# A fused attention and expert layer on one core: layer norm with features on the partitions from the third group on, and the probabilities' transposes one step later

## The reference, cut to what matters

```python
def _layernorm(x, axis=-1, eps=1e-05):
    m = jnp.mean(x, axis=axis, keepdims=True)
    v = jnp.var(x, axis=axis, keepdims=True)
    return (x - m) / jnp.sqrt(v + eps)
...
    h = jax.nn.relu(x @ nm_w1 + nm_b1)
    m = h @ nm_w2 + nm_b2
    return _sliding_window_attention(m, q_w, q_b, k_w, k_b, v_w, v_b, WINDOW_SIZE)
...
    scores = jax.nn.sigmoid(gates.astype(jnp.float32))
    sel_scores = scores + expert_bias
    _, inds = jax.lax.top_k(sel_scores, K)
...
    hg = jnp.einsum('bsd,eid->bsei', x, w_gate)
    hu = jnp.einsum('bsd,eid->bsei', x, w_up)
    h = jax.nn.silu(hg) * hu
    ye = jnp.einsum('bsei,edi->bsed', h, w_down)
    y = jnp.einsum('bsed,bse->bsd', ye, combine).astype(x.dtype)
...
    xn = _layernorm(x, axis=-1)
    x = x + _L0_attn_ref(xn, ...) + _L0_ffn_ref(xn, ...)
```

## Time and profile before

| | before |
|---|---|
| median of 3 runs | 727.82 us (727.58 to 728.45) |
| the profiled execution: own time | 727.74 us |
| the profiled execution: span | 725.9 us |
| granted TensorE clock | 0.999 of full speed |
| PE busy | 705.1 us (97% of the span) |
| DVE busy | 574.0 us (79%) |
| ACT busy | 439.1 us (60%) |
| POOL busy | 400.5 us (55%) |
| DMA | 84.72 MB, mean 117 GB/s |

### The profile page before, as it was taken

The page is one execution under the profiler, slowest core; times in us unless marked ns, Lnnn a source line. Parts: engine busy times, 40 slices in busy tenths (PEclk is TensorE's granted clock), DMA queues, the critical chain, the costliest instruction groups (busy, mean ns, idle before and its releaser), DMA issues.

```text
span 725.9 us, 10617 instructions
## 1 busy us (share of the span) xinstructions
PE 705.1 (97%) x3384; PEld 576.6 (79%) x3384; DVE 574.0 (79%) x1605; ACT 439.1 (60%) x874; POOL 400.5 (55%) x356
## 2 busy tenths in 40 slices
PE   5889999999999999999999999999999999999997
PEld 4667888788887888888788887888888788888886
DVE  5788788777888878788877888878787877888775
ACT  3575665656656565665656556566655656656573
POOL 3745555546565455555556564555565555655463
PEclk9999999999999999999999999999999999999999
DMA  7705316061240615215061240616225061430600
GB/s 254 258 5 169 110 30 220 29 233 44 95 184 2 232 45 182 96 46 215 18 234 44 110 168 4 231 45 200 78 50 221 8 234 45 127 137 7 243 1 15
DMA packets 36647, 84.72 MB, mean 117 GB/s; under 512 B 7152, under 2 KB 15472, under 8 KB 36592
## 3 DMA queue, kind: packets, MB, share of 16 engines
q1 hardware_dynamic: 36592, 84.05, 33.2%
HBM read 79.32 MB, written 4.72 MB: 116 GB/s over the span
## 4 chain that ended last, share of the span: by engine, by line
PE 79%; ACT 13%; DVE 4%; issue 2%; DMA 2%; POOL 0%; SPq 0%; DVEq 0%
PE ps_g L370 22%; PE ps_y L390 22%; PE ps_u L380 22%; ACT prob L553 4%; PE bank L306 3%; PE bank L348 3%; ACT L564 3%; ACT L528 2%; ACT silu L564 2%; PE bank L318 2%; PE bank L311 2%; DVE ps_u L889 2%; PE bank L329 1%; PE ps_y L357 1%; ACT h_hi L572 1%
## 5 line engine op out<-in xcount | busy, mean ns | idle before, releaser
L969 POOL TENSOR_TENSOR silu_c<-silu,comb_b 128x512 f32<-128x512 f32 x256 | 331.3, 1297 | 305.6 <-ACT silu L564 302.1
L572 ACT ACTIVATE h_hi<-ps_u 128x512 fp32r<-128x512 f32 x272 | 162.4, 597 | 267.3 <-DVE ps_u L889 267.3
L895 DVE TENSOR_TENSOR h_lo<-ps_u,h_hi 128x512 fp32r<-128x512 f32 x272 | 185.6, 682 | 59.9 <-ACT h_hi L572 59.6
L889 DVE TENSOR_TENSOR ps_u<-silu_c,ps_u 128x512 f32<-128x512 f32 x256 | 176.6, 690 | 50.3 <-PE ps_u L380 44.0
L564 ACT ACTIVATE silu<-ps_g 128x512 f32<-128x512 f32 x272 | 161.5, 594 | 0.2
L380 PE MATMUL ps_u<-xn_hi,exp_w_hi 128*128 128x512 f32 x272 | 110.7, 407 | 5.0 <-DVE h_lo L895 5.0
L390 PE MATMUL ps_y<-h_hi,exp_w_hi 128*128 128x512 f32 x272 | 112.6, 414 | 0.4 <-DVE h_lo L895 0.4
L370 PE MATMUL ps_g<-xn_hi,exp_w_hi 128*128 128x512 f32 x272 | 109.8, 404 | 2.1 <-ACT silu L564 0.6
L370 PE MATMUL ps_g<-xn_lo,exp_w_hi 128*128 128x512 f32 x272 | 108.0, 397 | 0.0
L370 PE MATMUL ps_g<-xn_hi,exp_w_lo 128*128 128x512 f32 x272 | 107.6, 396 | 0.0
L380 PE MATMUL ps_u<-xn_lo,exp_w_hi 128*128 128x512 f32 x272 | 107.4, 395 | 0.0
(11 more groups left out here) (139 smaller groups left out, 980.6 us busy)
## 6 DMA issues: line engine op xcount, KB each, us to landing
comb_b<-c_dram SPq DMA_DIRECT2D x64, 1024.0 KB, 8.5
xin<-x SPq DMA_DIRECT2D x16, 256.0 KB, 3.1
xres<-x_t SPq DMA_DIRECT2D x16, 256.0 KB, 2.6
out_t<-xres SPq DMA_DIRECT2D x16, 256.0 KB, 2.0
exp_raw<-wexp SPq DMA_DIRECT2D x3, 960.0 KB, 9.7
c_dram<-comb_t SPq DMA_DIRECT2D x64, 8.0 KB, 1.8
exp_raw<-wexp SPq DMA_DIRECT2D x1, 384.0 KB, 5.7
att_raw<-watt SPq DMA_DIRECT2D x1, 330.5 KB, 3.3
```

Source lines behind the costliest of these rows:

```text
L572: A(h_t[hbuf(par, s)][0][:], ps_u[(par + s) % 2][:], ACT.Copy).then_inc(s_h_hi, 1)
L889: V.tensor_tensor(ps_u[i][:], src[:], ps_u[i][:], ALU.mult).then_inc(s_h, 1)
L895: V.tensor_tensor(t[1][:], ps_u[(par + s) % 2][:], t[0][:].bitcast(F32), ALU.subtract)\
L969: G.tensor_tensor(silu_c[i][:].rearrange("p (l x) -> p l x", l=2), silu[i][:].rearrange("p (l x) -> p l x", l=2), comb_b[:, :, s1 - 1, :], ...
```

## The change

From the third group on (`TURNED = 2`), `xn` is no longer transposed by TensorE. SyncE loads the group's columns of `x_t` (the input already transposed in memory) straight into `xn`, and the two moments of each token, made as before with tokens on the partitions, are stored to memory (`st_dram`) and read back spread over all 128 partitions (`mom_b`). GpSimd then subtracts the mean in two halves of 256 tokens (`centre`) and multiplies by the inverse deviation (`normalise`), in place. For these groups the four `xn` transposes of TensorE and VectorE's four `normalise` instructions are gone, and `xn_hi` and `xn_lo` read `xn` in SBUF instead of `bank1` in PSUM. The load of `x` takes four neighbouring tokens for each partition.

The work for the moments is placed earlier: `moments` at step 5 (was 12), `variance` with a copy of the means at step 10 (was 14), `inverse_std` at step 10 behind that step's `silu_c`. SyncE stores and spreads the moments at step 11, ahead of the routing weights' store and spreads at step 13. `centre` is at the ends of steps 14 and 15, `normalise` at step 16.

Apart from that, for all groups, `turn_probs(0)` goes from the end of step 7 to step 8 behind down(5), `turn_probs(1)` from step 9 to step 10, and `prob_hi` with them; `prob_lo` of the second sequence goes from step 10 to step 11.

```diff
+            def load_turned(g):
+
+                if g == TURNED:
+                    sp.wait_ge(S["xn_tp"], g)
+                else:
+                    sp.wait_ge(S["xn_lo"], g)
+                sp.dma_start(flat(xn), x_t[:, g * T:(g + 1) * T]).then_inc(s_xt, 16)
+
+            def spread_moments(g):
+                n = g - TURNED + 1
+                sp.wait_ge(S["rstd"], g + 1)
+                sp.wait_ge(S["mean"], n)
+                sp.dma_start(st_dram.rearrange("k (p a) -> p k a", p=P), mom[:]).then_inc(s_mom_st, 16)
+                sp.wait_ge(s_mom_st, 16 * n)
+
+                if n > 1:
+                    sp.wait_ge(S["xn"], g)
+                sp.dma_start(mom_b[:], st_dram.rearrange("(o k) t -> o k t", o=1).to_broadcast([P, 2, T]))\
+                    .then_inc(s_mom_b, 16)
...
-                        sp.wait_ge(S["xn"], g + 1)
+                        sp.wait_ge(S["xn"] if g < TURNED else S["bn"], g + 1)
                         load_x(g + 2, par)
+                        load_turned(g + 2)
+                if s == 11 and not last(g, 1):
+                    spread_moments(g + 2)
...
-                if s == 1 and more:
+                if s == 1 and g + 1 < TURNED:
                     pe.wait_ge(S["xn"], g + 2)
...
-                if s == 9:
+                if s == 8:
+                    pe.wait_ge(S["pn0"], g + 1)
+                    turn_probs(0)
+                if s == 10:
                     pe.wait_ge(S["pn1"], g + 1)
                     turn_probs(1)
...
-                if s == 7:
-                    pe.wait_ge(S["pn0"], g + 1)
-                    turn_probs(0)
...
+                if g >= TURNED:
+                    n = g - TURNED
+                    if n > 0:
+                        dve.wait_ge(s_mom_st, 16 * n)
+                    V.tensor_copy(mom[:, 0, :], mv[:, :, 0]).then_inc(S["mean"], 1)
...
-                V.tensor_tensor(xn_t[par][1][:], bank[1][:], xn_t[par][0][:].bitcast(F32), ALU.subtract)\
+                V.tensor_tensor(xn_t[par][1][:], bank[1][:] if g < TURNED else flat(xn), xn_t[par][0][:].bitcast(F32), ALU.subtract)\
...
-                if s == 0 and more:
+                if s == 0 and g + 1 < TURNED:
                     normalise(g + 1, 1 - par)
...
+            def centre(g, half):
+                n = g - TURNED + 1
+                if half == 0:
+                    pool.wait_ge(s_xt, 16 * n)
+                    pool.wait_ge(s_mom_b, 16 * n)
+                c = slice(half * T // 2, (half + 1) * T // 2)
+                G.tensor_tensor(flat(xn)[:, c], flat(xn)[:, c], mom_b[:, 0, c], ALU.subtract)\
+                    .then_inc(S[f"centred{half}"], 1)
+
+            def normalise(g):
+                n = g - TURNED + 1
+                pool.wait_ge(S["centred0"], n)
+                pool.wait_ge(S["centred1"], n)
+                G.tensor_tensor(flat(xn), flat(xn), mom_b[:, 1, :], ALU.mult).then_inc(S["xn"], 1)
```

More of the change, by code:

```diff
@@ L46 @@
 NH = 4
+TURNED = 2
 EARLY = 8
@@ L62, in hdist, with layer @@
     return next(d for d in range(1, 2 * STEPS + 1) if order[(p - d) % (2 * STEPS)] == order[p])
-def layer(nc, x, x_t, watt, watt_t, expert_bias, wexp, out_t, c_dram):
+def layer(nc, x, x_t, watt, watt_t, expert_bias, wexp, out_t, c_dram, st_dram):
     ctx = ExitStack()
@@ L102, in layer @@
         xn = sb("xn", [P, TILES, P])
+        mom = sb("mom", [P, 2, TILES])
+        mom_b = sb("mom_b", [P, 2, T])
         xn_t = [[sb(f"xn_hi{i}", [P, T], F32R), sb(f"xn_lo{i}", [P, T], F32R)] for i in range(2)]
@@ L154, in layer @@
         s_xres = [sem(f"xres_loaded{i}") for i in range(2)]
+        s_xt = sem("x_t_loaded")
+        s_mom_st = sem("moments_stored")
+        s_mom_b = sem("moments_spread")
         s_const0 = sem("const_cleared")
@@ L189, in layer @@
         s_stored = [sem(f"y_stored{i}") for i in range(2)]
-        names = """bn aggr var_eps rstd xn xn_tp xn_hi xn_lo gate_mm gate_s gate_e
+        names = """bn aggr var_eps rstd mean centred0 centred1 xn xn_tp xn_hi xn_lo gate_mm gate_s gate_e
             gate_1 score select top8 rest weight wsum winv comb comb_t
@@ L233, in load_x @@
             def load_x(g, par):
-                sp.dma_start(xin[par][:], x[g * T:(g + 1) * T, :].rearrange("(a p) d -> p a d", p=P))\
-                    .then_inc(s_xin[par], 16)
+                rows = x[g * T:(g + 1) * T, :]
+                rows = rows.rearrange("(a p) d -> p a d" if g < TURNED else "(p a) d -> p a d", p=P)
+                sp.dma_start(xin[par][:], rows).then_inc(s_xin[par], 16)
+            def load_turned(g):
[14 more added lines that the diff above has]
+                    .then_inc(s_mom_b, 16)
             def load_res(g, par):
@@ L522, in xn_hi @@
             def xn_hi(g, par):
-                act.wait_ge(S["xn_tp"], g + 1)
-                A(xn_t[par][0][:], bank[1][:], ACT.Copy).then_inc(S["xn_hi"], 1)
+                if g < TURNED:
+                    act.wait_ge(S["xn_tp"], g + 1)
+                else:
+                    act.wait_ge(S["xn"], g + 1)
+                A(xn_t[par][0][:], bank[1][:] if g < TURNED else flat(xn), ACT.Copy).then_inc(S["xn_hi"], 1)
             def gate_exp(g):
@@ L847, in att @@
                     row_max(g, 0)
-                if s == 5 and more:
-                    gate_sum(g + 1)
+                if s == 5:
+                    if more:
+                        gate_sum(g + 1)
+                    if more2:
+                        moments(g + 2, par)
                 if s == 6:
@@ L862, in att @@
                 if s == 10:
+                    if more:
+                        route_sum(g + 1)
+                    if more2:
+                        variance(g + 2)
+                if s == 11:
                     prob_lo(g, 1)
                     if more:
-                        route_sum(g + 1)
-                if s == 11 and more:
-                    route_weights(g + 1, 1 - par)
-                if s == 12 and more2:
-                    moments(g + 2, par)
-                if s == 14:
-                    if more2:
-                        variance(g + 2)
-                    if more:
-                        hid_lo(g + 1)
+                        route_weights(g + 1, 1 - par)
+                if s == 14 and more:
+                    hid_lo(g + 1)
                 if s == 16:
@@ L927, in inverse_std @@
                 pool.wait_ge(S["var_eps"], g + 1)
-                G.tensor_tensor(rstd[:], var_eps[:], power[:], ALU.pow).then_inc(S["rstd"], 1)
+                if g > TURNED:
+                    pool.wait_ge(s_mom_st, 16 * (g - TURNED))
+                dst = rstd[:] if g < TURNED else mom[:, 1, :]
+                G.tensor_tensor(dst, var_eps[:], power[:], ALU.pow).then_inc(S["rstd"], 1)
+            def centre(g, half):
[11 more added lines that the diff above has]
+                G.tensor_tensor(flat(xn), flat(xn), mom_b[:, 1, :], ALU.mult).then_inc(S["xn"], 1)
             def prologue():
@@ L972, in slot @@
                 elif not last(g, 1):
+                    normalise(g + 2)
+                if s == 10 and not last(g, 1):
                     inverse_std(g + 2)
+                if s == 14 and not last(g, 1):
+                    centre(g + 2, 0)
+                if s == 15 and not last(g, 1):
+                    centre(g + 2, 1)
                 if s == 2:
@@ L1010 @@
     c_dram = nc.dram_tensor("c_dram", (2, 2 * E, 2, P), F32, kind="Internal").ap()
-    layer(nc, *args, out_t, c_dram)
+    st_dram = nc.dram_tensor("st_dram", (2, T), F32, kind="Internal").ap()
+    layer(nc, *args, out_t, c_dram, st_dram)
     r = run_bass_kernel_spmd(nc, [arrays], core_ids=[0])
```

## The result

The changed kernel takes 733.23 us in the median of 4 runs (732.35 to 733.75), the kernel before 728.13 us (727.58 to 728.62) on the same chip: a ratio of 1.0069, 95% interval [1.0052, 1.0086]. It is slower by 0.7%, under half of the 1.5% that I forecast. The profiled execution took 732.35 us with a span of 730.6 us. That is 4.61 us over the 727.74 of the profile before, where my sum says 11.1.

What follows compares the result with a forecast made beforehand. TensorE was taken as the limit, except 7.5 us a group that ScalarE sets before gate(9). Terms -6.2 + 3.3 + 6.2 + 0.3 + 6.4 + 1.1 = +11.1 us on 727.74 gave 738.8 us, range 726 to 743.

Steps and rivals of the forecast that it cites:

- The stretch that ScalarE sets: End of up(4) to gate(9): 7.5 us set by ScalarE; TensorE work inside is free if removed, costs full length if moved out.
- Part 1: Step 1 on TensorE: the four xn transposes go, 0.44 us in each of 14 groups, -6.2 us.
- Part 2: down(0) waits for finish_group on VectorE (ps_y for xres): 0.23 us in each of 14 groups, +3.3 us.
- Part 3: turn_probs(0) moved behind down(5) costs 0.44 us in 14 groups, +6.2 us, last group +0.3; turn_probs(1) costs nothing.
- Part 4: VectorE, steps 10 to 12: the pow holds comb, up(12) loses 0.49 us in 13 groups, +6.4 us; group 0 adds +1.1.
- rival B: Step 11: the pow, on 4 elements only, doesn't hold comb; +3.9 us, 731.6 us; chance 0.23.
- Rival C: Step 10: silu_c also holds the copy of the means, some 1.4 us a group, +12.3 us more, 751 us; chance 0.13.
- 0.6 us are covered: moments at step 5: a load of x landing up to 0.6 us late was priced at nothing.
- rival D: At up(8): moved turn_probs(0) costs nothing since TensorE waits for h_lo(6) anyway; 725, or 721.5 us; chance 0.10.

Runs made afterwards that it cites:

- e9: e8 with both turnings of the probabilities, their copies and prob_lo(1) back at the steps of the kernel before; 721.46 us, ratio 0.9905.
- e10: e9 with down(5) ahead of gate(9), and prob_lo(0) and prob_lo(1) moved from steps 9 and 10 to 12 and 13; 720.52 us.
- e11: e9 with down(5) ahead of gate(9) alone; 721.23 us, ratio 0.9896.
- e12: e9 with turn_probs(1), its copy and prob_lo(1) one step later again; 726.23 us, ratio 0.9961.
- e13: e4 with turn_probs(1) and its copy back at step 9, prob_lo(1) left at step 11; 727.51 us, ratio 0.9984.
- e4: The changed kernel with turn_probs(0) and prob_hi(0) back at step 7 and xn_lo at step 3; 727.64 us, ratio 0.9986.
- e8: e3 with the statistics earlier: moments at step 6, variance at 7, inverse_std at 8, spread_moments at 9; 727.10 us, ratio 0.9981.
- e3: The changed kernel with xn_lo at step 3 instead of step 2; 727.99 us, ratio 0.9997.
- e1: The changed kernel with turn_probs(0) and prob_hi(0) put back at step 7; 732.84 us, ratio 1.0063.
- e2: The kernel before with only turn_probs(0), behind down(5), and prob_hi(0) moved to step 8; 734.78 us, ratio 1.0088.
- e6: The changed kernel with an extra 128x384 GpSimd subtraction between silu_c(11) and the pow; 738.81 us, ratio 1.0145.
- e7: The changed kernel with the four aggregations of the moments computed a second time, into a spare tile, ahead of the real ones; 751.42 us, ratio 1.0313.

## Why the prediction was right or wrong

One table of the traces holds nearly all of it, with the distances (us) between the starts of up(4), gate(9) and up(12) in the group around 335 to 375 us (later in the slower ones), and the period:

| kernel | turning 0 | turning 1 | statistics | up(4) to gate(9) | gate(9) to up(12) | period |
|---|---|---|---|---|---|---|
| before | early | early | step 14 | 8.38 | 10.33 | 43.40 |
| e9 | early | early | early | 8.38 | 10.31 | 42.88 |
| e10, down(5) first, prob_lo late | early | early | early | 8.77 | 9.82 | 42.80 |
| e11, down(5) first | early | early | early | 8.78 | 9.92 | 42.89 |
| e12 | early | late | early | 8.37 | 10.68 | 43.24 |
| e13 | early | early | late | 8.38 | 10.68 | 43.36 |
| e4 | early | late | late | 8.38 | 10.67 | 43.35 |
| e8 | late | late | early | 8.38 | 10.70 | 43.28 |
| e3 | late | late | late | 8.38 | 10.75 | 43.35 |
| after | late | late | late | 8.38 | 10.72 | 43.60 |
| e1 | early | late | late | 8.39 | 10.68 | 43.60 |
| e2 | late | early | step 14 | 8.39 | 10.77 | 43.84 |
| e6 | late | late | late | 8.39 | 11.08 | 44.01 |
| e7 | late | late | late | 8.38 | 12.03 | 45.00 |

**The stretch that ScalarE sets** is as long as before, whatever stands in it: 8.37 to 8.39 us in every kernel that leaves down(5) behind gate(9) (the prediction's 7.5 us count from the end of up(4), these from its start). That was the view on which the prediction hung, and it holds.

**Part 1 and Part 2** were right. Outside the two columns the period is 43.40 - 18.71 = 24.69 us before and 43.60 - 19.10 = 24.50 after: -0.19, where I had -0.44 + 0.23 = -0.21. e3 takes Part 2 out, and has 24.22: the whole 0.44 is there, to 0.03 (e9 has 24.19, and e13, with the statistics late, 24.30).

**Part 3** was right in size (0.44 a group in e2) and incomplete in two ways. It gives turn_probs(1) at nothing, because steps 9 and 10 both lie outside the stretch; e12 has it cost 0.36 us a group alone. Counted from gate(9), up(9) starts at 3.96 us in the kernel before, with turn_probs(1) ahead of it. Without those transposes it would be TensorE's turn at 3.5, but h_lo(7) ends at 3.83, and up(9) starts at 3.88 in e12. So at step 9 turn_probs(1) fills some 0.37 us in which TensorE would wait. In the changed kernel turn_probs(0), behind down(5), fills the same gap (up(9) at 4.02), which is why nothing was lost there: each of the two hides the absence of the other.

The second way is how the costs combine. My sum has two terms, Part 3's 0.44 and Part 4's 0.49, as if each could be had back by itself. They belong to two lists that run side by side, and the longer one counts (Part 4 did compare them, 363.83 and 364.21, so the sum itself is not double). In the changed kernel both lists have grown without any hold of `comb`: from gate(9) to up(12) TensorE's is 10.7 us long by the turnings, and VectorE's, to the end of h_lo(10), is 10.6 by the statistics, where it was 10.0. This changed no number of mine, but it is why e1 gives back nothing.

**Part 4 is the step that failed**: "If the `pow` holds `comb` as `silu_c` does", "so I take the hold", +6.4 us, and 0.8 more in group 0. `comb` took 0.22 us beside the `pow` in all groups, and up(12) lost 0.06 us. That is rival B, whose condition I had named and given 0.23. The rest of Part 4 was right: on the clock of before (2.58 us off), `comb` starts at 362.54 (I had 362.59) and h_lo(10) ends at 363.68 (I had 363.73 without the hold). B's argument, that the `pow` works on 4 elements, fits what the runs show; the argument against it, that `comb` was held in all groups, had another neighbour in its rows. e6 shows that a wide instruction in that place does hold `comb`. That its 738.81 us meet my 738.8 is luck: its period grows by 0.61 us where my terms make 0.72 (0.23 and 0.49), and an odd group, which I don't have, makes up for part of it. The forecast of "slower" was right by Parts 2 and 3 alone, and the range held the measured time as B's, not as mine.

The Trainium skill, SBUF — State Buffer, section Who interferes with whom, on which this step leaned, has a VectorE instruction with two SBUF inputs contend with a GpSimd instruction that reads SBUF. It agrees with e6 (0.62 us) and doesn't agree with `comb` beside the `pow` (0.22 us in 14 groups); there the measurement decides. The same section lets `tensor_scalar` contend in a two-port mode; e7's 1.27 us for the addition agrees.

**Rival C** was no stray thought: e7 has its 1.4 us a group and its 751 us, by the neighbour of the instruction that I had named (C starts from the forecast with the hold of `comb`, so that the two totals meet is in part luck). The change keeps clear of it: the copy starts 0.15 us ahead of the product (I had summed 0.12).

**From B's 731.6 to the profiled 732.35** the terms are these. B has 14 x 0.23 us for the groups, and 14 x 0.19 were measured (-0.6). Two terms that B lacks are no step of the change: the odd group (+0.8), and the slow start of group 0 (0.83 up to the first full group where B has 0.3, +0.5). The end makes the rest. The median of the four executions, 733.23, lies another 0.9 above the profiled one, and no trace shows why. The odd group is a late load of `x`. VectorE waited for it:

```profile
306.10 0.87 DVE L687 BATCH_NORM_STATS2 stats<-xin 128x6 f32<-128x128 f32 x4 [1.43 <-DMA xin<-x]
...
312.06 0.50 PE L404 MATMUL ps_g<-xn_hi,exp_w_hi 128*128 128x512 f32 x1 [1.03 <-ACT silu L601]
```

The landing took 4.5 us instead of 3.1; I had written that 0.6 us are covered, and 1.43 - 0.78 = 0.65 were. What I didn't price is that one of 14 is later than that. Before, `moments` at step 12 had eight steps of cover. The other term is in group 0: windows of the changed kernel and of the one before (us, busy us of each engine, granted clock, DMA share, GB/s):

```profile
49.90:53.70 3.80, 3.72 (x9) 2.94 (x10) 3.76 (x14) 2.37 (x6) 1.28 (x1) 0.55 0.00 0
```

```profile
49.90:53.70 3.80, 3.65 (x18) 2.99 (x19) 3.76 (x14) 1.97 (x4) 1.29 (x1) 1.00 0.00 0
```

The changed kernel does half as many products here, at a granted clock of 0.55, near the lower of the two levels (1.2 GHz). Up to up(11) of group 0, e6 has the same instructions and the full clock: it starts up(11) at 57.39, the changed kernel at 58.35. So the low clock costs about 1 us there.

**The gain that I left on the table.** The normalisation on GpSimd and the two transfers cost nothing that a trace shows (no wait for `mom_b` in the lists of any). What costs are three moves that come with it: `xn_lo` ahead of `finish_group` (3.5 us), the turnings and the statistics into the 10.3 us behind gate(9) (6.5 us together, e3 against e9). e9 leaves all three out and is 7.2 us (0.95%) faster than the kernel before. My rival D had the size, 721.5, from a false reason.

## What to carry to other kernels

Before adding up the costs of several moved pieces, ask which list each one lengthens. Between the same two meeting points the longer list counts, so two costs there don't add, and undoing one of them shows nothing: e1 alone would have acquitted turn_probs(0), e12 and e13 together show why it didn't. When a bound rests on one engine holding another, the neighbour in the row must be of the same width and operation as the one in question; if it isn't, give the two cases even odds and let a kernel with another neighbour decide. And look for small instructions that start just ahead of another engine's wide one: in e7 a start 0.27 us later beside it made 1.27 us of 0.17, in 13 groups.

## What the runs showed of the hardware that I had not expected

- A `tensor_scalar` of 128x4 that starts 0.04 us after GpSimd's 128x512 product takes 1.27 us instead of 0.17 (e7), in 13 groups. One that starts 0.07 us ahead of such a product takes 0.17 (e8 to e12).
- A `pow` of 128x4 lasts 1.04 us on GpSimd and lets a VectorE instruction with two SBUF inputs pass at its bare 0.22 us; a subtraction of 128x384 that lasts 1.01 us doesn't (0.62). Whether the width or the operation makes the difference isn't shown.
- Behind a stop of TensorE in group 0 (near 50 us) the granted clock falls to the lower level in some executions, at once or about 1.5 us later (e12). All five profiled kernels with a stop of 2.8 to 3.8 us there (e8 2.81, e9 and e12 3.25, e10 3.76, e11 3.75) show it; of the nine with 2.25 to 2.69 us three do (the changed kernel 2.26, e1 and e13 2.69) and six don't (the kernel before 2.67, e4 2.69, e2, e3, e6 and e7 2.25 to 2.26). What decides among those nine stays open.
- Loads of `x` land later than usual once or a few times in an execution (the changed kernel, e1, e3, e4, e6, e7 and e13: 2 to 6 waits of VectorE for `x` in an execution, the longest 1.0 to 1.4 us); where VectorE takes them up a step later (e8 to e12), no wait for `x` is in the list.
